# Four PSUM banks for the sums of a graph-attention edge loop, on one Trainium2 core

## The reference

```python
left = jnp.einsum('eht,et->eh', el[src], mask)
right = jnp.einsum('eht,et->eh', er[dst], mask)
em_e = jnp.einsum('eht,et->eh', em, mask)          # em = e_pro (16 features) x attn_m
e = (left + right + em_e) / 3.0
e = jnp.where(e > 0, e, NEG_SLOPE * e)
e_max = jax.ops.segment_max(e, dst, num_segments=N)
e_exp = jnp.exp(e - e_max[dst])
e_sum = jax.ops.segment_sum(e_exp, dst, num_segments=N)
msg = feat_src[src] * (e_exp / e_sum[dst])[:, :, None]
rst = jax.ops.segment_sum(msg, dst, num_segments=N)
```

## Time and profile before

| | us |
|---|---|
| time, median of 3 runs | 4086.85 (4086.71 to 4087.13) |
| the profiled execution's own time | 4127.28 |
| its span | 4125.6 |
| POOL's gathers of the edge loop, first to last start | 314.0 to 2925.2 |
| the experts' tiles | about 3300 to 4125 |

### The profile page before, as it was taken

The page is one execution under the profiler, slowest core; times in us unless marked ns, Lnnn a source line. Parts: engine busy times, 40 slices in busy tenths (PEclk is TensorE's granted clock), DMA queues, the critical chain, the costliest instruction groups (busy, mean ns, idle before and its releaser), DMA issues. The chain is left out here.

```text
span 4125.6 us, 59259 instructions
## 1 busy us (share of the span) xinstructions
PE 3054.4 (74%) x12566; PEld 2356.6 (57%) x12567; DVE 1979.3 (48%) x5348; ACT 1623.2 (39%) x3631; POOL 1857.8 (45%) x1906
## 2 busy tenths in 40 slices
PE   3541777776777777777677776777765999999997
PEld 1221666565556665665566655555553677777775
DVE  6730555555555555555555555555673122222221
ACT  2311544454455444545544544455432222222221
POOL 0005456666666665666665666666254111111111
PEclk9865677777777777777767778777855999999998
DMA  7834444444444444444444444446564312121123
GB/s 221 258 138 112 123 140 130 131 128 129 131 129 130 131 130 128 132 138 130 130 131 129 130 130 130 130 129 119 75 216 136 91 31 32 31 32 31 31 32 83
DMA packets 309415, 481.35 MB, mean 117 GB/s; under 512 B 161911, under 2 KB 237507, under 8 KB 300366
## 3 DMA queue, kind: packets, MB, share of 16 engines
q0 software_dynamic: 100848, 285.40, 28.1%
q1 hardware_dynamic: 194910, 181.82, 14.5%
q10 hardware_dynamic: 13392, 11.23, 0.9%
HBM read 408.52 MB, written 76.12 MB: 117 GB/s over the span
## 5 line engine op out<-in xcount | busy, mean ns | idle before, releaser
L819 POOL DMA_INDIRECT rows<-table,idx x1664 | 1575.6, 947 | 1063.3 <-issue 445.9
L862 PE MATMUL ps_acc<-rows,hot 128*128 128x264 f32 x3328 | 1260.7, 516 | 538.5 <-DVE acc L1163 496.5
L862 PEld LDWEIGHTS ps_acc<-rows,hot 128*128 128x128 f32 x3328 | 761.9, 253 | 673.1 <-issue 566.6
L1163 DVE TENSOR_TENSOR acc<-acc,ps_acc 128x264 f32 x832 | 355.3, 427 | 987.3 <-remote 659.3
L847 PEld LDWEIGHTS ps_term<-er,hot_t 128*128 128x128 f32 x3328 | 638.1, 247 | 218.5 <-issue 146.5
L847 PE MATMUL ps_term<-er,hot_t 128*128 x3328 | 579.5, 305 | 85.7 <-issue 67.9
L1149 DVE TENSOR_TENSOR rows<-rows,ps_p 128x512 f32<-128x512 f32 x832 | 565.5, 680 | 3.8 <-ACT ps_p L971 0.5
L960 ACT ACTIVATE hot<-iota_row,neg_rel 128x128 f32<-128x128 f32 x1664 | 546.3, 388 | 8.7 <-PE ps_acc L862 8.0
L1730 PE MATMUL ps_h<-w,acc 128*128 x1680 | 528.5, 457 | 0.5 <-ACT acc L1649 0.5
L1642 POOL DMA_INDIRECT x_dram<-acc,to x105 | 161.7, 1540 | 761.8 <-ACT acc L1658 761.8
L935 ACT COPY e_t<-ps_e 128x128 f32<-128x128 f32 x208 | 56.4, 271 | 1021.6 <-remote 978.1
(11 more groups left out here) (263 smaller groups left out, 2811.9 us busy)
## 6 DMA issues: line engine op xcount, KB each, us to landing
dst_row<-rel_d SPq DMA_DIRECT2D x52, 1024.0 KB
rows<-table,idx POOLq DMA_INDIRECT x1664
rec<-rec_d SPq DMA_DIRECT2D x832, 24.0 KB
rec_d<-acc SPq DMA_DIRECT2D x16, 1050.0 KB
acc<-slots_x SPq DMA_DIRECT2D x105, 130.0 KB, 2.1
acc<-in_edge_attr_dram SPq DMA_DIRECT2D x16, 700.0 KB
wrow<-in_L_ffn_w_dram ACTq DMA_DIRECT2D x16, 640.0 KB
table<-fo SPq DMA_DIRECT2D x49, 148.0 KB
```

Of the source, the lines that this page charges most:

```text
L819: pool.indirect_dma_start(rows[:, in_ring(k) + j, :], None, table, bass.IndirectOffsetOnAxis(ap=idx[w][:, t:t + 1], axis=0)).then_inc(gath ...
L862: last = pe.matmul(ps_acc[m % 2][:, 0:PW], hot[m // QI % 2][:, m % QI * G + j, :], rows[:, in_ring(i * (2 * NI) + at) + j, 0:PW], start=(j ...
L1163: dve.tensor_tensor(so_far, so_far, ps_acc[m % 2][:, 0:PW].rearrange("p (h d) -> p h d", h=HEADS), ALU.add).then_inc(added, 1)
```

## The change

It has four parts.

1. **Four banks of sums.** `ps_acc` has `SUM_BANKS = 4` banks. PE's sum of an item waits on `added` of the item four earlier in place of two.
2. **Additions two steps later.** `ADD_LAG` is 27 in place of 25: DVE adds an item three steps after PE has summed it, not one.
3. **The chain of maxima in one bank.** `x_at` and `back_at` are the same columns 256 to 511 of `ps_l`; `ps_x` is gone. `less` is made at the start of `tops`, not at its end.
4. **Edge features a quad sooner.** PE turns the features of quad `v+3` at u = 1, behind that step's sum, into columns 384 to 511 of `ps_acc[1]`; `ps_e16` is gone. ACT copies them at u = 3, ahead of the one-hot's end. The copy waits on a new semaphore `edges_ps` (the edge term two quads back has been formed) in place of `term_ps`. DVE's additions out of bank 1, one in four, also wait on `e16_sb`, the copy's semaphore, since the bank is shared.

```diff
-ADD_LAG = 25
+ADD_LAG = 27
+SUM_BANKS = 4
+E16_STEP = 1
+E16_AHEAD = 3
...
-            x_at = ps_x[:, 0:ITEM]
-            back_at = ps_x[:, ITEM:2 * ITEM]
+            x_at = ps_l[:, ITEM:2 * ITEM]
+            back_at = x_at
+            e16_at = ps_acc[E16_STEP][:, 512 - P:512]
...
-                        after(pe, added, k1 - 2)
+                        after(pe, added, k1 - SUM_BANKS)
...
-                                if u == 1 and is_quad(i, at2):
-                                    turn_e16(i, at2, s2, r2)
                                 at, m = item(w, v, u, -SUM_LAG)
                                 if is_item(i, at):
                                     sums(i, at, m)
+                                if u == E16_STEP and is_quad(i, at3):
+                                    turn_e16(i, at3, s3, r3)
...
-                        after(act, term_ps, k1 - 2)
-                        act.copy(e16_t[s % 2][:, :], ps_e16[:, 0:P]).then_inc(e16_sb, 1)
+                        after(act, edges_ps, k1 - 2)
+                        act.copy(e16_t[s % 2][:, :], e16_at).then_inc(e16_sb, 1)
...
                                 if u == 1 and is_quad(i, at2):
-                                    copy_e16(i, at2, s2)
                                     compare(i, at2, s2, r2)
...
+                                if u == QI - 1 and is_quad(i, at4):
+                                    copy_e16(i, at4, s4)
                                 if u == QI - 1 and is_quad(i, at3):
                                     one_hot(i, at3, s3)
...
+                        if at % SUM_BANKS == E16_STEP:
+                            dve.wait_ge(e16_sb, min((k1 - 1) // QI + SUM_LAG // QI + E16_AHEAD + 1, BATCHES * QUADS))
                         dve.wait_ge(acc_done, k1)
```

More of the change, by code:

```diff
@@ L680, in gnn_moe_kernel @@
             scale = sb(st, "scale", [P, HEADS])
-            ps_e16 = ps(st, "ps_e16", [P, 512])
             ps_p = ps(st, "ps_p", [P, 512])
             ps_term = [ps(st, f"ps_term{u}", [P, 512]) for u in range(2)]
-            ps_acc = [ps(st, f"ps_acc{u}", [P, 512]) for u in range(2)]
-            ps_x = ps(st, "ps_x", [P, 512])
+            ps_acc = [ps(st, f"ps_acc{u}", [P, 512]) for u in range(SUM_BANKS)]
             ps_l = ps(st, "ps_l", [P, 512])
-            x_at = ps_x[:, 0:ITEM]
-            back_at = ps_x[:, ITEM:2 * ITEM]
+            x_at = ps_l[:, ITEM:2 * ITEM]
+            back_at = x_at
+            e16_at = ps_acc[E16_STEP][:, 512 - P:512]
             p_at = ps_p[:, 0:BT * HEADS].rearrange("p (e h) -> p e h", h=HEADS)
@@ L720, in gnn_moe_kernel @@
                  "less_ok", "scale_ok", "rescaled", "msg_ok", "square_ok", "hot_ok", "acc_done", "added", "e3_const"))
-            pen_ok = sem("pen_turned")
+            pen_ok, edges_ps = sem("pen_turned"), sem("edges_ps")
             rec_in, dst_row_in, pen_in = ([sem(f"{n}{w}") for w in range(2)] for n in ("rec_in", "dst_row_in", "pen_in"))
@@ L830, in turn_e16 @@
                         after(pe, e16_sb, k1 - 1)
-                        pe.transpose(ps_e16[:, 0:P], e16[s // QUADS][:, s % QUADS * QT:(s % QUADS + 1) * QT, :].rearrange("p t f -> p (t f)"),
+                        pe.transpose(e16_at, e16[s // QUADS][:, s % QUADS * QT:(s % QUADS + 1) * QT, :].rearrange("p t f -> p (t f)"),
                                      ident[:, :]).then_inc(e16_ps, 1)
@@ L858, in sums @@
                         pe.wait_ge(hot_ok, i * (2 * QUADS) + (at // QI + 1))
-                        after(pe, added, k1 - 2)
+                        after(pe, added, k1 - SUM_BANKS)
                         for j in range(G):
-                            last = pe.matmul(ps_acc[m % 2][:, 0:PW], hot[m // QI % 2][:, m % QI * G + j, :], rows[:, in_ring(i * (2 * NI) + at) + j, 0:PW],
+                            last = pe.matmul(ps_acc[(k1 - 1) % SUM_BANKS][:, 0:PW], hot[m // QI % 2][:, m % QI * G + j, :], rows[:, in_ring(i * (2 * NI) + at) + j, 0:PW],
                                              start=(j == 0), stop=(j == G - 1))
@@ L903, in slot @@
                             at1, s1, r1 = quad(w, v, 1)
-                            at2, s2, r2 = quad(w, v, 2)
+                            at3, s3, r3 = quad(w, v, E16_AHEAD)
                             for u in range(QI):
@@ L1003, in slot @@
                             at3, s3, _ = quad(w, v, -5)
+                            at4, s4, _ = quad(w, v, E16_AHEAD)
                             for u in range(QI):
@@ L1127, in tops @@
                         dve.wait_ge(carry_ps, batches(i, w, 1, 1))
+                        dve.wait_ge(first_ok, batches(i, w, 1, 1))
+                        after(dve, scale_ok, batches(i, w, 1))
+                        dve.tensor_scalar(less[:, :], drop_at, first[:, :], None, ALU.mult).then_inc(less_ok, 1)
                         step(dve.tensor_tensor(picked[:, :, :], carry_at, item_sel[:, :].unsqueeze(1).to_broadcast([P, 2, NI]), ALU.mult))
@@ L1132, in tops @@
                                                ALU.add, ALU.max).then_inc(tops_ok, 1)
-                        dve.wait_ge(first_ok, batches(i, w, 1, 1))
-                        after(dve, scale_ok, batches(i, w, 1))
-                        dve.tensor_scalar(less[:, :], drop_at, first[:, :], None, ALU.mult).then_inc(less_ok, 1)
                     def below_top(i, w):
@@ L1161, in add @@
                             dve.wait_ge(rescaled, n1)
+                        if at % SUM_BANKS == E16_STEP:
+                            dve.wait_ge(e16_sb, min((k1 - 1) // QI + SUM_LAG // QI + E16_AHEAD + 1, BATCHES * QUADS))
                         dve.wait_ge(acc_done, k1)
-                        dve.tensor_tensor(so_far, so_far, ps_acc[m % 2][:, 0:PW].rearrange("p (h d) -> p h d", h=HEADS), ALU.add).then_inc(added, 1)
+                        dve.tensor_tensor(so_far, so_far, ps_acc[(k1 - 1) % SUM_BANKS][:, 0:PW].rearrange("p (h d) -> p h d", h=HEADS), ALU.add).then_inc(added, 1)
                     def slot(i, w):
```

2 lines of the change are left out of this document (1 added, 1 removed).

## The result

The changed kernel takes 4045.36 us (median of 4 runs, 4042.06 to 4053.12), the kernel before in the same measurement 4086.78 us (4084.76 to 4087.13). The ratio is 0.9895, with an interval of 0.987 to 0.992: 41 us less, where 110 were forecast. The sign is right and the time lies in the range, but the forecast was 2.7 times too large.

The account below looks back on a forecast made before the run. Prediction: POOL's gathers plus pauses from late PE semaphores bound the loop. One more item a pause gave 114 us less, the end 4 more: 110 off 4086.85, so 3977 us; range 3845 to 4150.

Parts of the forecast that it names:

- What bounds the kernel: Loop: POOL's own gathers, 2.50 us an item, plus a 1.88 us pause each 3.24 items: 3.08 against 3.11 measured.
- holds: On PE: its semaphores come 2 to 4 us after its recorded ends, then all at once; cause not known.
- the whole term of 0.58 us: POOL's pauses in the loop, 0.580 us an item; 483 us less if all went.
- One more item for each pause: PE's sums with four banks: 4.24 items a pause in place of 3.24, 114 us less.
- The pause's length: POOL's pauses in the loop: kept at 1.88 us each, fewer but not shorter.
- the slower rival: DVE's wait at the shared bank delays weighing and sums; longer POOL pauses, first price 4149 us; slower had chance 0.16.
- The first rival: PE is let go only once POOL has stopped and its last gather landed; no change, 4087 us, chance 0.18.
- The holds set the pace: Same as The first rival: each hold costs POOL a pause whatever PE has issued; 4087 us, chance 0.18.
- The clock falls: PE in the loop at the lower clock, 1.2 GHz: gain ends at 83 us, 4004 us, chance 0.10.
- The new wait binds: DVE's wait for ACT's copy moves the next sums 0.3 us a quad: 62 us, 4149 us; slower, chance 0.16.
- The copy a quad sooner: ACT's comparison and mark run in the hold, ahead of the copy; nothing added beside the banks' term.
- The end: After the last items: additions end two steps later, 4 us more.

Follow-up runs that it names:

- e5: The change unaltered, against the kernel before, in a group without holds: 3573.36 us, ratio 0.9993.
- e15: Kernel before with three banks, additions one step later, features in their own bank two quads ahead, chain in one bank; all gathers, with holds: 4117.56 us, ratio 0.9956.
- groups 3 and 6: Two follow-up measurement groups, on chips 10 and 15, both with holds; the unaltered kernel before took 4119.89 and 4136.03 us.
- e14: e15's kernel with each item's second gather left out and its rows cleared once: 3339.35 us, 0.8176 of the whole kernel before.
- e11: Kernel before with each item's second gather left out and the rows cleared once: 3423.94 us, 0.8365 of the whole kernel before.
- e12: The change with each item's second gather left out and the rows cleared once: 3371.65 us, 0.8247 of the whole kernel before.
- e13: Kernel before plus only sooner features and copy (own bank) and one-bank chain, each item's second gather left out: 3420.54 us, 0.8369 of the whole kernel before.

## Why the prediction was right and wrong

**What bounds the kernel: right, for the groups that have holds.** POOL's issue plus a pause per so many items gives 2.50 + (278.3 / 109 - 0.30) / 4.58 = 2.99 us an item for the change, against 3.00 measured; 4.58 is 332 + 334 + 333 gathers / 2 / 109 pauses. The same sum gave 3.08 against 3.11 before. With the pauses of the timeline it is closer still: 2.50 + (339.5 / 150 - 0.30) / 3.21 = 3.11 us before and 2.50 + (281.6 / 101 - 0.30) / 4.93 = 3.00 us in the change. That the 149 waits of the prediction come so near the 150 pauses is luck: 15 of them are of 0.30 to 0.32 us, and 16 real pauses stand under "issue". e5 shows the 2.50 bare. What the prediction couldn't know is that the pause is not there in other groups, where the whole term of 0.58 us, and any gain on it, is nothing.

**One more item for each pause: the number moved as foretold and further, but mostly not by the holds.** 4.24 was forecast, 4.58 came, from 3.24. PE's waits for additions fell to a third, where "nearly gone" was foretold, and 333 gathers in 500 us stand beside the "about 334". But the sum counted all pauses as holds, and the two kinds moved differently. Less 0.30 us each, the short ones cost (55.3 - 42 x 0.30) / 482 = 0.089 us an item before and (10.9 - 8 x 0.30) / 498 = 0.017 in the change, where 482 and 498 are the items of the stretch. Over 832 items that is 60 us less, and 62 less in e15. The long ones, worked out in the same way, cost 29 us less in the change and 44 more in e15. So most of what was gained in these profiles are the pauses that came between the holds, and both kernels with more banks have it. That it is PE's third sum that no longer waits there fits the order of things at 1508.30 to 1510.40, and is not shown apart.

**The pause's length: the step that failed.** The sum kept 1.88 us a pause ("POOL's pauses fewer, not shorter") and had longer ones only as a sign of the slower rival. They cost 2.25 us. With 1.88 and the 4.58 items that came, an item would take 2.910 us; with 2.25 it takes 2.991. The difference, 0.081 x 832 = 67 us, is what the longer pauses took back.

By the timeline the mean pause grew from 2.26 to 2.79 us, and for two reasons of about equal weight. The short ones went out of the mean, which alone makes 2.53 of it. And the long ones grew from 2.63 to 2.91 us.

The first rival said that a hold ends only some 2 us after POOL's last gather (it read 1.9 and 2.0, the rows give 2.03 and 1.95). The releases fit it: 1.83 to 2.47 us in the five shown, and the medians 1.92, 1.94 and 2.29. If POOL isn't let go before it has stopped, whatever PE has issued, banks can't shorten such a pause, only put off the stop. In the change the release comes 0.37 us later, which is enough for the 0.28 us by which its long pauses grew, but why it comes later stays open. It is hardly that PE is still at work, in instructions 1.40 us apart as in the hold shown: the 25 long pauses in which no PE instruction starts before the release last 2.85 us in the mean, the other 68 last 2.93. The prediction's account of a hold was too narrow as well: it has PE's semaphores 2 to 4 us late, where its own second hold, from 1514.59 to 1523.31, makes it 8.7.

**The base of the sum was not the usual execution.** The pauses were counted in an execution 40 us above its median, and 110 us were then taken off the median as they stood. Of the 69 us that were missing, the profiles against each other account for 25 (85 in place of 110). The other 44, the larger part, is that 85 between two profiles is 41 between medians. Whether the profile of before is an unusual execution or one on a chip where this kernel always takes longer (groups 3 and 6 have 4119.89 and 4136.03 us), the record doesn't say. So some of what differs between the two profiles, the counts of pauses too, may be such a difference and not the change. e15's profile stands nearer to that of before in this, and has the short pauses gone as well.

**The three rivals on the other terms.** "The holds set the pace" is half right: its mechanism is in every hold shown, and e15 comes near its outcome, with holds as often as before and a gain of 0.4%. In the change POOL met 93 holds for 108, so its outcome, no gain, fell. "The clock falls" is refuted: it is 0.76 to 0.79 where it was 0.75 to 0.76, and 0.93 in e14 with three banks where e11 has 0.87. The Trainium skill's rule in TensorE: Matmul & The Clock Gate, section "A second HAM failure mode: psum-queue depth-cycling", tells of a kernel whose cycling through PSUM banks left small gaps and a clock that went up and down. These runs don't bear it out as a price of more banks: the measurement decides, and here four banks had 0.76 to 0.79 for 0.75 to 0.76 with all gathers, and four and three had 0.90 and 0.93 for 0.87 with half of them. "The new wait binds" fell as an outcome. But both of its signs came: POOL's pauses are longer, and DVE stands idle for the copy, 17 times 2.6 us in 1500 us of the change and 28 times 2.5 us in e12. That is far longer than the 0.3 us that the sum gave an uncovered wait, which I had covered by "its own sum is three steps old". What it costs the change with all gathers was not measured apart; in e12 it may be the 32 us to e14. (Its price for 1 us is 208 us, so 4295 and not 4290.)

**The copy a quad sooner: nothing, as forecast, where it could be told.** e13 against e11 shows it with half of the gathers. With all gathers and holds it was not run alone. There the change did better against its own group (0.9895) than three banks did against theirs (0.9956), and the difference of the two profiles lies in the long pauses alone, 93 for 118. In e15 PE waits behind the held copy, which the change moved. That the copy pays only together with the banks would fit both. It is open, as are the fourth bank and the second step, since no group with holds had both kernels whole.

**The end.** The forecast gave 4 us more there. The span fell 85.1 us and the stretch of gathers 79.4, with a start 0.8 us later, so what lies after them got some 6 us shorter. Why is not known.

## What to carry to other kernels

When a rate is "issue plus a pause for each so many items", both numbers of the pause move: an edit that puts the stop off may also lengthen it, and what ends the pause must be known before its length is kept. Sort the pauses by length before their mean goes into a sum: here two kinds of pause stood in one mean, and the change took away the one and little of the other. Freeing the wait that is named first is not the same as freeing the engine: three banks took 275 of 293 us of PE's waiting away and only 17 of the 339.5 us for which POOL paused. And take a profile's pauses off the median only after asking whether that execution is a usual one.

## What was not expected of the hardware

The same program took 3574 us in some groups of runs and 4087 to 4136 in others, each steady within its group, and both on a chip of the same number some 11 minutes apart. Without holds POOL made its gathers without a pause (400 in 500 us). With them semaphores of PE came late to ACT, DVE and POOL (8.7 us in the hold from 1514.59, with waits of up to 9.6 us), every 12 to 18 us, and mostly about 2 us after POOL had stopped. With half of the gathers the same loop had next to no such waits, in groups where the whole kernel, by its time, has them. So the change's 41 us are a gain on a condition of the chip and not on the kernel's work: where it is absent, the two kernels can't be told apart (0.9993 and 0.9999). What makes the condition isn't known from these runs.

No kernel here beats the change at whole work in a shown way. Three banks with features in their own bank were 1.0% ahead with half of the gathers, and behind, by ratios of different groups, with all.
